# Second cross-attention core: split scores, and P times V spread over the next head's query blocks

## The reference, cut to what matters

```python
q = rms_norm(x @ q_w + q_b, nq_s).reshape(B, S, H, D)            # B=2, S=512, H=16, D=128
k_img = rms_norm(img_ctx @ ki_w + ki_b, nki_s)                   # keys 0 to 256
k_txt = rms_norm(txt_ctx @ k_w + k_b, nkt_s)                     # keys 257 to 1023
out = softmax(q k_img^T / sqrt(D)) v_img + softmax(q k_txt^T / sqrt(D)) v_txt
return out.reshape(B, S, H * D) @ o_w + o_b
```

## Time and profile before

| | us |
|---|---|
| median of 3 runs | 3708.18 (3707.67 to 3718.57) |
| span of the profiled execution | 3699.9 |
| of it `attention_core1`, first score matmul to the output projection | 2239.0 to 2835.2 |
| PE busy / DVE busy / ACT busy / POOL busy | 3211.2 / 1407.2 / 1068.2 / 1211.0 |

### The profile page before, as it was taken

The page is one execution under the profiler, slowest core; times in us unless marked ns, Lnnn a source line. Parts: engine busy times, 40 slices in busy tenths (PEclk is TensorE's granted clock), DMA queues, the critical chain, the costliest instruction groups (busy, mean ns, idle before and its releaser), DMA issues. The chain is left out here.

```text
span 3699.9 us, 46093 instructions
## 1 busy us (share of the span) xinstructions
PE 3211.2 (87%) x14270; PEld 2008.5 (54%) x14270; DVE 1407.2 (38%) x2706; ACT 1068.2 (29%) x2408; POOL 1211.0 (33%) x1245
## 2 busy tenths in 40 slices
PE   7898978888855969897996998999999946999997
PEld 3564434434344854565885884555554432677773
DVE  3473345545440120674344225555552131011114
ACT  1351154444310101443332003444442000222220
POOL 2351035544402120551442104555553014222215
PEclk9899989999967989898998999999999957999998
DMA  2342031312006961433442434222220000999996
GB/s 77 69 100 85 23 69 34 66 36 60 12 25 226 318 202 44 101 81 101 147 137 102 140 114 138 73 71 71 71 71 20 18 24 3 340 344 342 341 323 186
DMA packets 312931, 444.32 MB, mean 120 GB/s; under 512 B 40638, under 2 KB 173990, under 8 KB 312840
## 3 DMA queue, kind: packets, MB, share of 16 engines
q1 hardware_dynamic: 282376, 371.83, 32.9%
q0 software_dynamic: 15488, 44.09, 3.8%
q10 hardware_dynamic: 14976, 27.27, 2.1%
HBM read 308.78 MB, written 75.58 MB: 104 GB/s over the span
## 5 line engine op out<-in xcount | busy, mean ns | idle before, releaser
L1326 PE MATMUL ps<-moe_blocks_xgt,moe_blocks_w 128*128 128x128 f32 (+1 forms) x3072 | 365.0, 277 | 6.7 <-DMA moe_blocks_b1s<-rb_cols 5.0
L1326 PEld LDWEIGHTS ps<-moe_blocks_xgt,moe_blocks_w 128*128 128x128 f32 (+1 forms) x3072 | 351.2, 185 | 11.0 <-issue 6.4
L2205 POOL TENSOR_TENSOR normed<-normed,xa_core_rinv 128x257 f32<-128x257 f32 (+1 forms) x256 | 266.1, 1062 | 273.0 <-DVE xa_core_rinv L2136 273.0
L416 PE MATMUL ps<-identity,normed 128*128 128x128 f32 x1664 | 273.8, 282 | 79.3 <-ACT xa_core_pt L519 41.5
L547 POOL TENSOR_TENSOR normed<-normed,xa_core_rinv 128x1024 f32<-128x1024 f32 x128 | 240.5, 1895 | 250.6 <-DVE xa_core_rinv L456 250.1
L1308 PE MATMUL ps<-moe_blocks_w,moe_blocks_ht 128*128 128x512 f32 (+1 forms) x624 | 284.9, 593 | 0.0
L416 PEld LDWEIGHTS ps<-identity,normed 128*128 128x128 f32 x1664 | 193.0, 143 | 143.3 <-issue 64.8
L2172 ACT ACTIVATE normed<-ps,xa_core_nmax 128x257 f32<-128x257 f32 (+1 forms) x256 | 173.8, 685 | 322.7 <-DVE xa_core_nmax L2131 322.2
L2131 DVE TENSOR_REDUCE xa_core_nmax<-ps 128x1 f32<-128x257 f32 (+1 forms) x256 | 164.5, 684 | 250.1 <-PE ps L2082 250.1
L2082 PE MATMUL ps<-xa_core_k,xa_core_q 128*128 128x512 f32 x512 | 243.8, 600 | 13.1 <-DVE xa_core_k L2121 11.1
L451 DVE TENSOR_REDUCE xa_core_nmax<-ps 128x1 f32<-128x1024 f32 x128 | 156.2, 1221 | 240.0 <-PE ps L392 239.6
(11 more groups left out here) (281 smaller groups left out, 5712.7 us busy)
## 6 DMA issues: line engine op xcount, KB each, us to landing
moe_blocks_w<-L_ffn_rw SPq DMA_DIRECT2D x80, 704.0 KB
moe_blocks_w<-L_ffn_rw SPq DMA_DIRECT2D x80, 512.0 KB
moe_blocks_w<-L_ffn_w SPq DMA_DIRECT2D x24, 1408.0 KB
sa_core_packed<-sa_core_parts SPq DMA_DIRECT2D x256, 128.0 KB, 2.4
moe_y<-moe_blocks_y ACTq DMA_DIRECT2D x104, 256.0 KB
xa_core_packed<-xa_core_parts SPq DMA_DIRECT2D x128, 128.0 KB, 2.3
k_raw<-xa_kq_raw SPq DMA_DIRECT2D x64, 256.0 KB, 2.0
v_rows<-normed SPq DMA_DIRECT2D x64, 256.0 KB
```

What stands on the lines that cost most here:

```text
L416: mm = nc.tensor.transpose(g.ps[:, t_bank(kk, half), n * P:(n + 1) * P], prob[:, kk % PR, j * P:(j + 1) * P], g.ident[:, :])
L1326: mm = nc.tensor.matmul(g.ps[0:fn, 2 + s % 2 + 2 * half, f * P:(f + 1) * P], w1s[s][:, k, half * F + f0:half * F + f0 + fn], xgt[:, s % 2, ...
L2205: ins = nc.gpsimd.tensor_tensor(prob[:, n % PR, lo:hi], prob[:, n % PR, lo:hi], rinv[:, n % PR, m:m + 1].to_broadcast([P, hi - lo]), ALU.mult)
```

## The change

In `project_kq1`, ACT writes each unit from PSUM a second time: keys with the per-feature gain in `k_out`, queries rounded to the high part in `q_high`; DVE subtracts for `q_low`. DRAM gets the gained keys and both parts of the queries (512 KB for a head in place of 256 KB). PE's and SP's waits go by `ready`, which comes after the second write. `rq` is laid down as one number for each query on its partition, made by eight one-column matmuls, one root and one reciprocal.

In the core, `k` is a single raw slot. POOL multiplies it by `rk` (`scale`), ACT rounds it to `k_high` (`high`), DVE subtracts for `k_low` (`low`); `k_high`, `k_low`, `q` and `v` have two slots. Scores are `split_matmul` on these. The queries' factor goes into the exponent's scale and into a small multiply of the maxima. P times V of a head is cut into four parts of two matmuls, one behind the scores of each of the steps 4j+7 to 4j+10 (before, all eight stood in step 4j+7 behind the transposes). The copies of the transposes move to the head of DVE's and ACT's step, one step later than before.

SP's list for head j is now: wait for `k_lows` of head j-1, k; wait for the scores of head j-2, q; wait for P times V of head j-2, v. POOL calls `scale` of head j+1 ahead of step 4j's probabilities; ACT calls `high` of head j+1 behind the exponentials of step 4j+1; DVE calls `low` of head j+1 at the end of step 4j+2.

```diff
-    k_dram = nc.dram_tensor("k_raw", (B * H, P, CTX), F32, kind="Internal").ap()
-    q_dram = nc.dram_tensor("q_raw", (B * H, P, S), F32, kind="Internal").ap()
+    k_dram = nc.dram_tensor("k_scaled", (B * H, P, CTX), F32, kind="Internal").ap()
+    q_dram = nc.dram_tensor("q_parts", (B * H, P, 2, S), F32, kind="Internal").ap()
...
-                    sp.wait_ge(done, UH * h + u + 1)
+                    sp.wait_ge(ready, UH * h + u + 1)
                     if u < 4:
                         b, half = divmod(u, 2)
-                        dst = k_dram[h + b * H, :, half * 512:(half + 1) * 512]
+                        sp.dma_start(k_dram[h + b * H, :, half * 512:(half + 1) * 512],
+                                     k_out[:, u, :]).then_inc(stored[u], 16)
                     else:
-                        dst = q_dram[h + (u - 4) * H, :, :]
-                    sp.dma_start(dst, raw[:, u, :]).then_inc(stored[u], 16)
+                        sp.dma_start(q_dram[h + (u - 4) * H, :, 0, :],
+                                     q_high[:, u - 4, :].bitcast(F32)).then_inc(stored[u], 16)
+                        sp.wait_ge(q_lows, 2 * h + u - 3)
+                        sp.dma_start(q_dram[h + (u - 4) * H, :, 1, :],
+                                     q_low[:, u - 4, :].bitcast(F32)).then_inc(stored[u], 16)
...
-                        pe.wait_ge(done, UH * h + u - UH + 1)
+                        pe.wait_ge(ready, UH * h + u - UH + 1)
...
+            for t in range(NT):
+                mm = nc.tensor.matmul(g.ps[:, 4, t:t + 1], sums[:, B * CTX + t * P:B * CTX + (t + 1) * P], g.ones[:, 0:1],
+                                      start=True, stop=True)
+            mm.then_inc(total, 1)
...
+                    if not (first and slot == 0):
+                        act.wait_ge(stored[u], (16 if u < 4 else 32) * h)
+                    for n, lo, hi in parts:
+                        bank = 6 + u // 2 if n == 0 else u
+                        if n < 2:
+                            ins = nc.scalar.activation(k_out[:, u, lo:hi], g.ps[:, bank, lo:hi], ACT.Identity,
+                                                       bias=gain[:, slot, 1, n:n + 1], scale=gain[:, slot, 0, n:n + 1])
+                        else:
+                            ins = nc.scalar.activation(q_high[:, u - 4, :], g.ps[:, bank, :], ACT.Identity,
+                                                       bias=bias[:, slot, n:n + 1])
+                    ins.then_inc(ready, 1)
                     if u == NEXT and not last:
...
+                    if u >= 4:
+                        dve.wait_ge(ready, UH * h + u + 1)
+                        if not (first and slot == 0):
+                            dve.wait_ge(stored[u], 32 * h)
+                        nc.vector.tensor_tensor(q_low[:, u - 4, :], raw[:, u, :], q_high[:, u - 4, :],
+                                                ALU.subtract).then_inc(q_lows, 1)
                     if u == NEXT and not last:
...
-    k = st.sbuf("k", [P, HP, CTX])
-    q = st.sbuf("q", [P, HP, S])
+    k = st.sbuf("k", [P, CTX])
+    k_high, k_low = st.sbuf("k_high", [P, HP, CTX], F32R), st.sbuf("k_low", [P, HP, CTX], F32R)
+    q = st.sbuf("q", [P, HP, 2, S], F32R)
     v = st.sbuf("v", [P, HP, NKT, DX])
...
-            def load(i, s, first=False):
+            def load(i, s):
                 j = HP * i + s
-                if not first:
+                if not isinstance(i, int) or j >= 1:
+                    sp.wait_ge(k_lows, j)
+                sp.dma_start(k[:, :], k_dram[j, :, :]).then_inc(k_loaded, 16)
+                if not isinstance(i, int) or j >= HP:
                     sp.wait_ge(scores, QB * (j - 1))
-                sp.dma_start(k[:, s, :], k_dram[j, :, :]).then_inc(kq_loaded[s], 16)
-                sp.dma_start(q[:, s, :], q_dram[j, :, :]).then_inc(kq_loaded[s], 16)
-                if not first:
+                sp.dma_start(q[:, s, :, :].bitcast(F32), q_dram[j, :, :, :]).then_inc(q_loaded[s], 16)
+                if not isinstance(i, int) or j >= HP:
                     sp.wait_ge(pv_done, j - 1)
                 sp.dma_start(v[:, s, :, :], v_dram[j, :, :, :].rearrange("t p d -> p t d")).then_inc(v_loaded[s], 16)
...
+                s, qb = divmod(n, QB)
+                if qb == 0:
+                    pe.wait_ge(k_lows, HP * i + s + 1)
+                    pe.wait_ge(q_loaded[s], 16 * i + 16)
+                if reaches(i, n - SB):
+                    pe.wait_ge(exp_done, u - SB + 1)
+                qs = slice(qb * P, (qb + 1) * P)
+                for c in range(0, CTX, 512):
+                    mm = split_matmul(nc, s_ps(n)[:, c:c + 512], q[:, s, 0, qs], q[:, s, 1, qs], k_high[:, s, c:c + 512],
+                                      k_low[:, s, c:c + 512], start=True, stop=True)
+                mm.then_inc(scores, 1)
...
+            def values(i, n):
...
+                head, part = divmod(n - SKEW, QB)
+                j, hs = HP * i + head - 1, (head - 1) % HP
+                if part == 0:
                     for half in range(2):
+                        pe.wait_ge(pt_done[half], QB * j + QB)
+                    pe.wait_ge(v_loaded[hs], 16 * (i + (head - 1) // HP) + 16)
+                    if not isinstance(i, int) or j >= HP:
+                        pe.wait_ge(ot_done, j - HP + 1)
+                for m in range(part * LOAD, (part + 1) * LOAD):
+                    mm = nc.tensor.matmul(g.ps[:, 6 + hs, :], v[:, hs, m, :], pt[:, hs, m, :], start=(m == 0),
+                                          stop=(m == NKT - 1))
+                if part == QB - 1:
...
+            def turn(i, n):
+                w, slot = U * i + n - SKEW, (n - SKEW) % PR
+                pe.wait_ge(prob_done, w + 1)
+                for half in range(2):
+                    if reaches(i, n - SKEW - 1):
+                        pe.wait_ge(pt_done[half], w)
+                    for m in range(4):
+                        c = (4 * half + m) * P
+                        mm = nc.tensor.transpose(g.ps[:, 4 + half, m * P:(m + 1) * P], prob[:, slot, c:c + P],
+                                                 g.ident[:, :])
+                    mm.then_inc(turned[half], 1)
+            def step(i, n, b, nb):
+                multiply(i, n)
+                if reaches(i, n - SKEW - QB):
+                    values(i, n)
+                if reaches(i, n - SKEW):
+                    turn(i, n)
...
+            def low(j, s):
+                dve.wait_ge(k_highs, j + 1)
+                nc.vector.tensor_tensor(k_low[:, s, :], k[:, :], k_high[:, s, :], ALU.subtract).then_inc(k_lows, 1)
...
+                    ins = nc.vector.tensor_reduce(peak[:, n % PR, m:m + 1], s_ps(n)[:, lo:hi], X_AXIS, ALU.max,
+                                                  negate=True)
+                ins.then_inc(peak_done, 1)
+                dve.wait_ge(peak_done, u + 1)
+                nc.vector.tensor_scalar(nmax[:, n % PR, :], peak[:, n % PR, :], rq[:, b * QB + n % QB:b * QB + n % QB + 1],
+                                        None, ALU.mult).then_inc(max_done, 1)
+                if reaches(i, n - 1):
+                    invert(i, n)
+                if n == 2:
+                    low(HP * i + 1, 1)
+                if n == QB + 2 and nb is not None:
+                    low(HP * i + 2, 0)
...
+            def high(j, s, i=None):
+                act.wait_ge(k_done, j + 1)
+                if reaches(i, s * QB - U):
+                    act.wait_ge(scores, QB * (j - 1))
+                nc.scalar.activation(k_high[:, s, :], k[:, :], ACT.Copy).then_inc(k_highs, 1)
...
+                if reaches(i, n - SKEW - 1):
+                    take(i, n)
+                act.wait_ge(max_done, u + 1)
+                if reaches(i, n - PR):
+                    for half in range(2):
+                        act.wait_ge(turned[half], u - PR + 1)
+                t = b * QB + n % QB
+                for m, (lo, hi) in enumerate(SPANS):
+                    ins = nc.scalar.activation(prob[:, n % PR, lo:hi], s_ps(n)[:, lo:hi], ACT.Exp,
+                                               bias=nmax[:, n % PR, m:m + 1], scale=rq[:, t:t + 1],
+                                               accum_out=rsum[:, n % PR, m:m + 1])
+                ins.then_inc(exp_done, 1)
+                if n == 1:
+                    high(HP * i + 1, 1, i)
+                if n == QB + 1 and nb is not None:
+                    high(HP * i + 2, 0, i + 1)
+                if n % QB == QB - 1 and reaches(i, n - U):
+                    store(HP * i + n // QB - 2, n // QB)
...
+            def scale(j, b):
+                pool.wait_ge(k_loaded, 16 * j + 16)
+                nc.gpsimd.tensor_tensor(k[:, :], k[:, :], rk[:, b * CTX:(b + 1) * CTX], ALU.mult).then_inc(k_done, 1)
...
+                if n == 0:
+                    scale(HP * i + 1, b)
+                if n == QB and nb is not None:
+                    scale(HP * i + 2, nb)
```

247 lines of the change are left out of this document (101 added, 146 removed).

## The result

| | before | after |
|---|---|---|
| median of 4 runs, us | 3711.16 (3707.67 to 3718.57) | 3966.77 (3961.47 to 3974.78) |
| span of the profiled execution | 3699.9 | 3972.9 |
| core, first scores to the output projection | 596.2 | 859.4 |

The ratio is 1.0687, with a 95% interval from 1.0669 to 1.0705. The prediction was 3979 us, from 3915 to 4035.

A forecast was written before the change was run, and what follows sets the result against it. PE was taken as the bound, busy 558 of 582 us in the core. Terms -81 + 5 + 2.5 - 6.4 + 2 = -78 and +349 for 29 stalls gave +271: 3708.2 + 271 = 3979 us, range 3915 to 4035.

The forecast's parts named there:

- Part 1: Work of a core head: shorter split scores, no half waits for ACT's copy in the transposes; 2.53 us less, 81 in all.
- idle on PE in a stall: Core, PE standing within the transposes while the next head's late k is loaded and converted: 9.7 us (9.0 to 10.5).
- clock behind a stall: Core, PE's work after each idle at half speed: 2.35 us lost each time (1.65 to 3.05).
- start of the core: First scores wait for a conversion on three engines, handovers and q instead of DVE alone: +2.5 us.
- last reciprocals of `project_kq1`: End of `project_kq1`: two 128x512 reciprocals with nothing on PE become one of eight columns: -6.4 us.
- its heads: Heads of `project_kq1`: unit 3's second write delays ACT's rounding of the next weights; +2 us, up to 8 if cover fails.
- ramp: First core heads: k of head 2 queued behind `wo`, POOL has scaling and probabilities in steps without P times V: +5 us.
- the rival with the keys in time: Core: k of head j+1 lands before POOL asks, leaving only the -78: 3630 us, chance 0.06.
- the rival without the clock: Core: PE stands 9.7 us a head but keeps its clock: 3926 us, chance 0.12.
- The 8.3 us: Whole program: the runs' median lies 8.3 us above the profiled span, added to go from span to forecast time.
- A longer stall: Core: DVE, ACT and POOL backlog makes PE wait a second time, 2.5 us more a head: 4052 us, chance 0.1.
- k land 2 us sooner: Core, shorter stall: k overtakes v in the queues and lands 2 us sooner: 3921 us, chance 0.07.

The follow-up runs named there:

- one change in SP's list: The changed kernel with k and q of head j+1 issued ahead of v of head j: 3624.59 us, ratio 0.9820; second run 3650.08 us.
- the filled idles: The changed kernel with 36 more matmuls behind the last part of P times V in each of the 29 stalling heads: 3900.55 us, ratio 1.0567.

## Why the prediction was right

It was right in sign, mechanism and size, and for the reason it gave: one change in SP's list takes the whole loss away and more. Part of the closeness of the number is luck, since its errors have both signs, and since the terms of Part 1 cannot be had apart (below).

| step, us | predicted | measured |
|---|---|---|
| a head with no stall | 15.79 | 16.15 |
| idle on PE in a stall | 9.7 (9.0 to 10.5) | 9.00 to 9.31 |
| clock behind a stall | 2.35 (1.65 to 3.05) | 2.1, of which 1.66 come back |
| stalls | 29 | 29 |
| a head with a stall | 27.8 | 27.33 |
| start of the core | +2.5 | +1.5 |
| last reciprocals of `project_kq1` | -6.4 | -5.5 |
| its heads | +2 | +1.9 |
| ramp | +5 (0 to 8) | +10 |
| the rival with the keys in time, against before | -78 | -72, -63 |

- *The chain.* Each link came as listed. Over the 29 stalls the way to k's issue is 0.95 (0.9 taken), the landing 4.69 (5.0, where the earlier trace rows had 4.7), POOL, ACT and the copy are within 0.1, and the three handovers come to some 0.15 (0.3). The sum was 10.1, the mean is 9.68.
- *The clock.* The earlier trace rows gave 3.3 to 6.1 us of work at the low clock behind an idle; here it is 4.2 to 5.2, and 2.1 are lost by it. What the clock is worth is less, 1.66, mostly for the wait of 0.2 to 0.4 that it hides. The prediction named that wait and priced the rival without the clock at 53 us less; the filled idles gave 1.66 x 29 = 48. The Trainium skill, "TensorE: Matmul & The Clock Gate", section "HAM oscillation — how this bites in real kernels", says that a loop that waits for a DMA in each turn starts each turn at the low clock. The trace agrees: the granted clock was 0.50 in the first 4 us behind this stall, 0.81 over the whole core, and 1.00 once the idles were filled.
- *The sum.* A head with a stall is 16.15 + 9.08 (the mean of the 29 idles) + 2.1 = 27.33. The core grew by 263.2 us, where -81, +5 and +349 had made 273. Idle and clock were 0.6 and 0.25 a stall too high, 25 us; against that the head without a stall was 0.36 too low, 12 us, and the ramp 5 (the last 2 are the old head, 18.37 and not 18.32). In that head a step's scores take 1.48 and not 1.36, its transposes 0.79 and not 0.87, and a short wait ahead of P times V stays in some steps.
- *The 8.3 us.* The prediction went from the span to the median by adding 8.3 us that were said to lie around the program. The runs show less: an execution of the changed kernel takes 1.8 to 2.4 us more than its span (3974.78 for 3972.9 in the profiled one, the slowest of the four), so most of the 8.3 was probably the difference between executions. The medians differ by 255.6, the two spans by 273.0. Of these 261 lie in the parts that changed and 12 elsewhere, 3.5 ahead of `project_kq1` and 8.3 behind the core (864.8 before, 873.1 after). The second trace of the changed kernel has 850.9 behind the core, so the 12 are hardly the change.
- *The small terms.* PE's idle ahead of the core is 12.62 us, before 11.07 (2227.9 to 2238.96); from the last projection matmul of `project_kq1` to the first of `project_v1` it is 32.6 and before 38.1; PE's part of `project_kq1` takes 273.5 and before 271.6. The ramp is the core's length less its heads: 8.4 before (596.2 - 32 x 18.37), 18.4 after (859.4 - 29 x 27.33 - 3 x 16.15). Of the latter 8.3 are PE's waits for exponentials and copies between 2245 and 2267, which I had taken for shorter.
- *The cases.* A longer stall did not come: the backlog of POOL (four multiplies, 5.01 us) is worked off beside PE. Nor did k land 2 us sooner: its landing is 4.4 to 5.0.

**Where my picture was incomplete.** Part 1 made the gain of 2.53 a head out of shorter scores (4 x 0.36) and half waits that go (about 1.1), as if they could be had apart. The runs say no. The rest of the change with a whole P times V, shorter scores included, is 1.5 us a head *slower* than before (19.89 for 18.37), and the spread without the rest 2.25 slower (20.62), keys in time both times; only together do they give 2.2 (16.15). A whole P times V covers the old conversions of the next head and starves the other engines; the spread evens the load. That what the spread needs is the new place of the conversions, and not the shorter scores, is likely from the idle above, but no run had the one without the other. That the sum for both was nearly right is no proof of its terms.

## What to carry to other kernels

When work that frees a buffer is moved later, read the list of the queue that refills it: every load behind that wait is late too, whether it needs the buffer or not, and here reordering two lines turned +6.9% into -1.8%. Price a stall as its chain of steps in a row. Where PE's granted clock falls in it, as it did here, add what the low clock costs behind it, less the waits that the slow stretch hides. Before spreading a long block over several steps, ask which conversions lay under it, and test parts of a change in pairs, since their gains need not add.
